# Turned down products in four experts stages, the recurrent layer's finish inside the cross attention, and query batches projected between first scores

## What is computed

```python
x = x + L0_attn(ln(x));  x = x + L0_xattn(ctx, ln(x), mask)      # "x0"
x = x + L0_ffn(ln(x))       # 8 experts, hidden 512, silu(gate) * up; "f0"
x = x + L1_attn(ln(x));  x = x + L1_xattn(ln(x), ctx)            # "x1"
x = x + L1_ffn(ln(x))       # one dense block, hidden 384, silu(gate) * up; "L1"
x = x + L2_attn(ln(x))      # recurrence over 512 steps, then ln(r) * gamma + beta
x = x + L2_xattn(ln(x), ctx, full mask)                          # "x2"
x = x + L2_ffn(ln(x))       # 8 experts, hidden 256, relu(g) * p, plus its own input; "f2"
x = x + L3_attn(ln(x));  x = x + L3_xattn(ln(x), ctx)
x = x + L3_ffn(ln(x))       # 8 experts, hidden 256, relu(x w1 + b1) w2 + b2; "f3"

# an expert: every token goes through every expert, the weight is 0 where it was not chosen
h  = act(x @ gate_w.T) * (x @ up_w.T)
eo = h @ down_w.T
out = out + coef[:, e] * eo
```

## Time and profile before

| | |
|---|---|
| median of 3 runs | 2433.44 us (2431.93 to 2447.59) |
| the profiled execution | 2440.75 us, span 2438.9 us |
| instructions | 36556 |
| PE | 2066.0 us, 85% of the span |
| DVE | 1662.4 us, 68% |
| ACT | 1045.7 us, 43% |
| POOL | 533.2 us, 22% |
| mean granted TensorE clock | 0.889 of full speed |

### The profile page before, as it was taken

The page is one execution under the profiler, slowest core; times in us unless marked ns, Lnnn a source line. Parts: engine busy times, 40 slices in busy tenths (PEclk is TensorE's granted clock), DMA queues, the critical chain, the costliest instruction groups (busy, mean ns, idle before and its releaser), DMA issues. The chain is left out here.

```text
span 2438.9 us, 36556 instructions
## 1 busy us (share of the span) xinstructions
PE 2066.0 (85%) x12192; PEld 1383.0 (57%) x12216; DVE 1662.4 (68%) x4273; ACT 1045.7 (43%) x2326; POOL 533.2 (22%) x905
## 2 busy tenths in 40 slices
PE   6698899998999897767774997598699979999888
PEld 3455788884555455433332554587334348777777
DVE  5666677786675576779997565456679856666655
ACT  2354222222564453455551344322367734444333
POOL 0342110102110530068883321010211010000010
PEclk8698899997897799889996798799689979999989
DMA  8321000004120420000003220000511110000000
GB/s 338 99 60 23 1 1 1 1 1 130 44 53 18 121 60 2 1 1 0 1 1 105 73 48 8 1 1 1 174 36 46 33 44 1 1 1 1 1 1 18
DMA packets 60073, 94.61 MB, mean 39 GB/s; under 512 B 11313, under 2 KB 33137, under 8 KB 58737
## 3 DMA queue, kind: packets, MB, share of 16 engines
q1 hardware_dynamic: 29312, 55.29, 6.7%
q0 software_dynamic: 29952, 36.45, 6.2%
q10 hardware_dynamic: 624, 0.54, 0.1%
HBM read 65.50 MB, written 31.29 MB: 40 GB/s over the span
## 5 line engine op out<-in xcount | busy, mean ns | idle before, releaser
L1008 DVE TENSOR_REDUCE m<-banks 128x1 f32<-128x512 f32 (+3 forms) x512 | 272.6, 584 | 94.6 <-PE banks L1172 54.4
L2687 PEld LDWEIGHTS banks<-w_ffn,eh 128*128 128x128 f32 x2144 | 279.2, 191 | 23.5 <-DVE eh L2628 1.9
L2687 PE MATMUL banks<-w_ffn,eh 128*128 128x128 f32 x2144 | 281.2, 274 | 1.5 <-DVE eh L2628 1.5
L1140 ACT ACTIVATE p<-banks 128x512 f32<-128x512 f32 (+3 forms) x512 | 234.0, 522 | 101.4 <-PE banks L1218 58.7
L1443 DVE TENSOR_REDUCE m<-banks 128x2 f32<-128x308 f32 x384 | 165.7, 475 | 137.1 <-PE banks L1743 70.3
L2675 PE MATMUL banks<-x_hi,w_hi 128*128 128x512 f32 x472 | 211.2, 447 | 17.4 <-PEq L332 17.4
L1170 PE MATMUL banks<-K,Qf 32*128 32x512 f32 (+2 forms) x512 | 182.5, 515 | 14.6 <-PEq L332 9.9
L2657 ACT ACTIVATE et<-banks 128x512 f32<-128x512 f32 x140 | 83.6, 597 | 246.8 <-PE banks L2677 203.2
L2677 PE MATMUL banks<-x_hi,w_lo 128*128 128x512 f32 x472 | 188.7, 400 | 0.0
L2676 PE MATMUL banks<-x_lo,w_hi 128*128 128x512 f32 x472 | 187.6, 397 | 0.0
L1216 PE MATMUL banks<-Q,K 32*128 32x512 f32 (+2 forms) x512 | 153.5, 499 | 14.9 <-ACT p L1140 13.0
(11 more groups left out here) (423 smaller groups left out, 4332.7 us busy)
## 6 DMA issues: line engine op xcount, KB each, us to landing
Qf<-stack_q_plain POOLq DMA_DIRECT2D x48, 256.0 KB, 3.0
Qf<-stack_q_masked POOLq DMA_DIRECT2D x32, 256.0 KB, 3.0
K<-stack_k_self POOLq DMA_DIRECT2D x32, 256.0 KB, 3.1
w_ffn<-ffn_dram SPq DMA_DIRECT2D x1, 6144.0 KB, 35.2
stack_q_plain<-q_hi SPq DMA_DIRECT2D x24, 256.0 KB, 3.1
stack_q_masked<-q_hi SPq DMA_DIRECT2D x16, 256.0 KB, 3.0
stack_k_self<-k_hi SPq DMA_DIRECT2D x16, 256.0 KB, 3.8
K<-stack_k_ctx POOLq DMA_DIRECT2D x48, 80.0 KB, 2.7
```

The source lines that it names most:

```text
L1008: ins = dve.reduce_max(k.m[:, t, h:h + 1], bank[:, 0:(t + 1) * P if k.kind == "page" else S], AX)
L1140: nc.scalar.activation(k.p[:, x % PBUFS, q0:S], score_banks[x % 3][:, q0:S], ACT.Exp).then_inc(sem("exp_done"), 1)
L2687: last = pe.matmul(bank[:, t * P:(t + 1) * P], k.h[:, n % RING, t * P:(t + 1) * P], w(down.format(e))[:, i * P:(i + 1) * P], start=(i == 0 ...
```

## The change

1. **Products turned.** In all experts stages `output(n)` takes the down weight as the stationary operand and h as the moving one, 512 tokens at once, with both split in a high and a low fp32r part: 3 matmuls an item. The sum over the tiles of a pair has the model dimension on partitions; ACT copies it out (`take_output`, in f3 with the bias as the activation's own), PE turns it back with 4 transposes into the same bank (`turn_output`), and DVE adds it to x. ACT writes the high part of h (`high`), GpSimd the low part (DVE in f3). GpSimd also cuts the down weights, and its cuts stand at fixed items among the low parts (`cuts`). The output lags 3 items instead of 2. The ring of split weights holds 2, 1, 4 and 3 experts; with two kinds and 2 tiles the hidden banks are 2 of each kind, not 3. In f2 the last 3 experts are taken batch by batch; L1 norms 1 batch ahead, not 2.
2. **Store by batch.** In f3 each batch is stored when its last expert has been added.
3. **The finish moved.** `scan_finish` is gone; in x2 GpSimd adds beta batch by batch and DVE multiplies and adds each batch before its norm (`add_scanned`).
4. **Later batches between first scores.** In all three cross attentions only batches 0 and 1 are normed before the first maximum; batches 2 and 3 are normed in pieces among the first maxima. PE turns batches 1, 2, 3 after chunks 1, 7, 13, projects 1 and 2 after chunks 4 and 10, and batch 3 after the chunks.

```diff
-        self.wring = 2 * tiles
+        self.wring = rings * tiles
+        self.d_hi, self.d_lo = sb("d_hi", [P, self.wring, P], F32R), sb("d_lo", [P, self.wring, P], F32R)
+        self.h_hi, self.h_lo = sb("h_hi", [P, HRING, S], F32R), sb("h_lo", [P, HRING, S], F32R)
...
+    def cuts(e, at):
+        if e >= apart:
+            return [(e + 1, at)] if lead == 1 and e == apart and at < tiles and e + 1 < experts else []
+        new = [(f, j) for f in range(1 if e == 0 else e + lead, e + lead + 1 + (e == apart - 1 and k.rings > 3)) if f < experts for j in range(tiles)]
+        late = 0 if e == 0 else 3
+        step = max(1, (B * tiles - late) // max(1, len(new)))
...
         @block.gpsimd
-            for e in range(1, experts):
-                cut_weights(net, pool, k, first, tiles, e, (e - 1) * tiles)
+            for i in range(tiles):
+                cut_down(net, pool, k, down, 0, i)
+            for n, (m, i) in enumerate(work):
+                if pool_lows:
+                    pool.wait_ge(sem("h_high"), n + 1)
+                    nc.gpsimd.tensor_tensor(k.h_lo[:, n % HRING], k.h[:, n % RING], k.h_hi[:, n % HRING].bitcast(F32), ALU.subtract).then_inc(sem("h_parts"), 1)
+                for new, j in cuts(e, b * tiles + i):
+                    cut_weight(net, pool, k, first, new, j, (new - 1) * tiles)
+                    cut_down(net, pool, k, down, new, j)
...
         @block.scalar          # for each item n, after the activation of item n
+                if n >= 1:
+                    high(n - 1)
+                if n >= TAKE and work[n - TAKE][1] == tiles - 1:
+                    take_output(work[n - TAKE][0])
...
         @block.tensor
-                for t in range(QT):
-                    last = pe.matmul(bank[:, t * P:(t + 1) * P], k.h[:, n % RING, t * P:(t + 1) * P], w(down.format(e))[:, i * P:(i + 1) * P],
-                                     start=(i == 0 and t == 0), stop=(i == tiles - 1), skip_group_check=True)
+                pe.matmul(y_bank[:], k.d_hi[:, at], h_hi, start=i == 0, stop=False)
+                pe.matmul(y_bank[:], k.d_lo[:, at], h_hi, start=False, stop=False)
+                pe.matmul(y_bank[:], k.d_hi[:, at], h_lo, start=False, stop=i == tiles - 1).then_inc(sem("h_used"), 1)
+            def turn_output(m):
+                pe.wait_ge(sem("y_taken"), m + 1)
+                for t in range(QT):
+                    last = pe.transpose(y_banks[m % ny][:, t * P:(t + 1) * P], k.y[:, t * P:(t + 1) * P], w("ident"))
-            for n in range(len(work) + 2):
+            for n in range(len(work) + LAG + 2):
                 if n < len(work):
                     hidden(n)
-                if n >= 2:
-                    output(n - 2)
+                if n >= LAG + 2 and work[n - LAG - 2][1] == tiles - 1:
+                    turn_output(work[n - LAG - 2][0])
+                if n >= LAG and n - LAG < len(work):
+                    output(n - LAG)
...
         # cross_block, DVE
+            if finish:
+                add_scanned(0)
             if not early:
                 vector_layernorm_of(dve, ch, net.x, k.n, 0, QT).then_inc(sem("xn_ready"), 1)
...
-            vector_layernorm_of(dve, ch, net.x, k.n, max(early, 1) * QT, B * QT).then_inc(sem("xn_ready"), 1)
+            if finish:
+                add_scanned(1)
+                vector_layernorm_of(dve, ch, net.x, k.n, QT, 2 * QT).then_inc(sem("xn_ready"), 1)
+                add_scanned(2)
+                ch.link(vector_layernorm_of(dve, ch, k.n.xn, k.n, (B - 1) * QT, B * QT))
+                add_scanned(3)
+            elif early <= 1:
+                vector_layernorm_of(dve, ch, net.x, k.n, QT, 2 * QT).then_inc(sem("xn_ready"), 1)
+            begun = max(early, 2)
...
                 maximum(c)
+                b, piece = divmod(c - 1, PIECES)
+                if 0 <= b < B - begun:
+                    vector_norm_piece(dve, ch, net.x, k.n, (begun + b) * QT, (begun + b + 1) * QT, piece)
...
         # cross_block, PE
-            normed(1)
-            project_queries(1)
             for c in range(nch + FIRST):
                 first_scores(c)
-                if c in (2, 7):
-                    normed(2 + c // 7)
-                if c in (5, 10):
-                    project_queries(2 + c // 10)
+                if c in (1, 7, 13):
+                    normed(1 + c // 6)
+                if c in (4, 10):
+                    project_queries(1 + c // 6)
+            project_queries(B - 1)
...
-        experts(None, None, "silu", ("L1_w", "L1_d"), 1, 3, norm_kind="one", ahead=2)
+        experts(None, None, "silu", ("L1_w", "L1_d"), 1, 3, rings=1, norm_kind="one", ahead=1)
...
-            scan_finish(net, k)
```

More of the change, by code:

```diff
@@ L1559, in values @@
                 pool.wait_ge(sem("v_ready"), (n + 1) * (GROUP + 1))
+            if finish:
+                for b in range(B):
+                    x = x_of(net, b)
+                    nc.gpsimd.tensor_tensor(x, x, over(w("m_beta"), 1, QT), ALU.add).then_inc(sem("with_offset"), 1)
             pool.memset(k.K[:, :, KPAD:].bitcast(F32), 0.0).then_inc(sem("zeroed"), 1)
@@ L2575, in experts_block @@
     pieces = DOUBLE_PIECES if norm_kind == "double" else PIECES
-    stretch = (experts - apart) * tiles
-    begin = apart * B * tiles + stretch + 2
+    stretch = max((experts - apart) * tiles, pieces)
+    begin = (apart * B + experts - apart) * tiles + LAG + 3
+    pool_lows = act_kind != "bias"
+    hidden_banks = 2 if tiles == 2 and k.kinds == 2 else 3
+    y_banks = ps[6:8] if tiles > 2 else ps[4:8]
+    ny = len(y_banks)
+    lead = min(2, k.rings - 1)
+    def cuts(e, at):
[4 more added lines that the diff above has]
+        step = max(1, (B * tiles - late) // max(1, len(new)))
+        c, rest = divmod(at - late, step)
+        return [new[c]] if rest == 0 and 0 <= c < len(new) else []
     with nc.Block() as block:
@@ L2631, in _ @@
-                if i == 1 and m >= 1:
-                    add_expert(m - 1)
-                b, piece = divmod(n - begin, max(stretch, pieces))
+                    hidden(n)
+                else:
+                    low(n)
+                if n >= LAG + 3 and work[n - LAG - 3][1] == tiles - 1:
+                    add_expert(work[n - LAG - 3][0])
+                b, piece = divmod(n - begin, stretch)
                 if 0 <= b < ahead and piece < pieces:
                     norm_piece(b, piece)
+            left = range((len(work) - LAG - 3) // tiles, len(pairs))
@@ L2645, in _, with high, take_output @@
         def _(act):
+            def high(n):
+                act.wait_ge(sem("h_ready"), n + 1)
+                if n >= HRING:
+                    act.wait_ge(sem("h_used"), n - HRING + 1)
+                nc.scalar.copy(k.h_hi[:, n % HRING], k.h[:, n % RING]).then_inc(sem("h_high"), 1)
+            def take_output(m):
+                act.wait_ge(sem("h_used"), tiles * (m + 1))
+                if m >= 1:
+                    act.wait_ge(sem("turned"), m)
+                e = pairs[m][0]
+                if act_kind == "bias":
+                    taken = nc.scalar.activation(k.y[:], y_banks[m % ny][:], ACT.Identity, bias=w("b2")[:, e:e + 1])
+                else:
+                    taken = nc.scalar.copy(k.y[:], y_banks[m % ny][:])
+                taken.then_inc(sem("y_taken"), 1)
             for n, (m, i) in enumerate(work):
```

218 lines of the change are left out of this document (120 added, 98 removed).

## The result

The changed kernel takes **2476.78 us** (median of 4 runs, 2461.78 to 2479.76) against 2432.68 of the kernel before in the same job: a ratio of **1.0155, 95% interval 1.0109 to 1.0202**. It is slower, by some 38 us by that ratio, which is worked out from all the runs; the two medians lie 44.1 us apart.

A forecast was written before the change was run, and what follows sets the result against it. PE was taken to bound the experts stages and first scores. Terms f0 +1.6, L1 and hand-over +2, f2 +9, f3 +25, x0 +10.5, x1 +7.5, x2 -3.8 gave +52 on 2433.4: 2485 us, range 2438 to 2508.

The forecast's parts named there:

- Part 2: In f3 PE waits at the turn for ACT's copy, 0.63 us a pair, +20 us; no wait in f0, L1, f2.
- Part 1: Turned product on PE, with four transposes a pair: f0 -6 us, L1 nothing, f2 +6, f3 +6.
- Part 3: GpSimd's cuts and low parts back up, so PE waits for the low part: f0 +2.8 us, f2 +2.5.
- Part 4: Stage ends: f0 +3.3 and +1.5 (norm pieces), f2 +0.4, f3 +1.4 and -2.3 (store), L1 hand-over +2 us.
- Part 5: Norm pieces, turns and projections among the first scores lengthen the cross attentions: x0 +10.5 us, x1 +7.5, x2 +7.
- Part 6: Finish moved into x2: its block's 13.3 us go, first scores begin 2.5 later; with x2's +7, -3.8 in all.
- no late turn: Rival: in f3 ACT starts its copy early enough, f3 pays 6 and not 26: 2465 us; chance 0.17.
- free turns: Rival: transposes vanish in PE's stream and ACT's copy is never waited for: 2409 us; chance 0.06.
- the slower product: Rival: the turned product is no faster than the old, 0.89 us an item: +51 us more; chance 0.03.
- First scores not set by DVE: Rival: only PE's added work counts, cross attentions give +1 in place of +14: 2472 us; chance 0.15.
- Norm pieces behind low parts: Rival: in f0's and f2's last quarter DVE's short operations wait for GpSimd: +20, 2505 us; chance 0.09.

The follow-up runs named there:

- run 3: The changed kernel, but in f3 ScalarE copies a pair's summed product before writing the high part of h: 2458.54 us, ratio 1.0103 against the kernel before.
- run 8: The kernel before with x2 alone changed (finish inside, later batches between first scores), store by batch, and L1 norming one batch ahead, not two: 2428.07 us.
- run 9: The kernel before once more, unedited, for a second profile: 2442.22 us.
- run 2: The changed kernel with batches 1 to 3 normed before the first maximum in all cross attentions, turns, projections and GpSimd's queue in changed order: 2468.30 us.
- run 10: The kernel before with f0's turned product, the finish inside x2 with later batches between first scores, and store by batch: 2425.88 us, ratio 0.9969.

## Why the prediction held, and where it did not

The forecast was 2485 and the sum +52; 2476.78 lies in the range, and the profile shows +39. So the sum is 13 too high, above all in f0 (+1.6 foreseen, -10.3 + 4.0 found) and f2 (+9 foreseen, +3.7 found), and terms too low elsewhere hide part of it. Step by step:

- **Part 2, the wait in f3**, is right in cause and size: 0.63 a pair foreseen, 0.66 measured in the pair above, and run 3 takes 15 us away by ACT's order alone.
- **Part 1, the pair's cost**, is mis-sized. It took 0.2325 for a matmul and 0.56 for the turn; measured are 0.227 and 0.41 + 0.08. (The 0.50 of the earlier trace rows ends at one more transpose, which has a wait of its own, so it can hold more than four transposes.) Made again: f0 36 x 0.227 + 0.49 = 8.66 against 9.12, f2 4.58 against 4.56, f3 3.21 against 3.17. So f0 -15 and not -6, f2 and f3 +1 and not +6 each. f0's -10.3 is that with 7.2 us of waits (next two steps), less 1.7 that the kernel before lost itself (291.3 against 31.75 x 9.12) and about 1 that I can't place; f2's +3.7 is nearly all waits, 1.7 and 1.9. The old item's price held the gaps of its own mix of matmuls, and I carried them into a stream that has none.
- **Part 3, GpSimd's backlog**: foreseen 2.8 and 2.5. In f0's steady part the waits of TensorE (line, releaser: us in total, times, longest) are

```profile
PE banks L2805 <- ACT ey L2741: 2.4, 2, 1.3
PE banks L2798 <- POOL h_lo L2650: 1.8, 3, 1.0
```

  These count from modelled ends and so come out low. By the starts of an item's last product (L2800), the items from 485.78 on, among the last cuts, take 2.47, 3.42 and 3.36 us in place of 2.04: the backlog costs 3.1 there, as foreseen, and 1.2 once more at f0's start. In f2 it costs 1.7. The two waits for the copy are not the backlog's, for they lie in the last expert, where GpSimd cuts nothing:

```profile
519.20 1.28 POOL L2650 TENSOR_TENSOR h_lo<-eh,h_hi 128x512 fp32r<-128x512 f32 x1 [0.77 <-ACT h_hi L2730]
519.30 1.21 DVE L406 TENSOR_TENSOR sq<-sq,vh 128x4 f32<-128x4 f32 x1
...
522.77 0.62 ACT L2730 CAST h_hi<-eh 128x512 fp32r<-128x512 f32 x1 [2.12 <-DVE eh L2694]
523.30 0.58 ACT L2741 COPY ey<-banks 128x512 f32<-128x512 f32 x1
...
523.93 0.66 PE L2805 MATMUL banks<-w_start,ey 128*128 128x128 f32 x4 [1.19 <-ACT ey L2741]
```

  A 4-element operation of a norm piece lasts 1.21 us and ends with GpSimd's low part; VectorE's next product for h is late, ACT waits 2.12 for it with the high part, and the copy that TensorE needs stands behind that. The second wait, at 542.70, looks the same. By item starts the two cost 2.9 us, where part 4 had 1.5 for the pieces and part 2 had said that f0 shows no wait for the copy.
- **Part 4**: f0's end +4.0 (foreseen +3.3). f3's end +0.4 (foreseen -0.9): the store gives 2.7 as said, but the chain costs 3.1, not 1.4. L1's +2 came, from the wrong cause: -1.5 for the batch and +3.6 for the product's end, for which I had put down nothing. Another 3.5 between L1 and x2 (-7.7 = -13.3 + 2.1 + 3.5) are the clock of run 8's windows and what follows them.
- **Part 5, first scores**: x0's stretch is 20.9 where 21.1 was counted (100.9 to 122.0), x1 +9.9 (foreseen +7.5: 6.5 in the stretch, the rest behind it), x2's stretch +6.5 (foreseen +7). In x0 the reason is right: VectorE is the path up to its last piece, and TensorE waits for it. That the end fits to 0.2 is luck: the last piece ends at 118.83 and not at 117.8, and turn, copy and projection behind it take 2.9 and not 4.2. (The earliest begin was also added wrongly, 97.41 + 2.7 is 100.1 and not 100.3; nothing hangs on it.)
- **Part 6**: the block was worth 13.3 to the tenth, x2 +8.8 (foreseen 9.5). The short operation behind GpSimd lasted 2.42, and the first scores begin 3.4 later (foreseen 2.5); that the memsets too stood in its way fits the rows above, but no run moves them.
- The stretch before f3 gave -5.4, which an unchanged kernel shows too (run 9), and no step had it. That much of a total read from one profile is luck.

Of the rivals, no late turn, free turns and the slower product are refuted: by 0.66 a pair, by 0.41 a turn, and by 2.04 an item. First scores not set by DVE is refuted by run 2 in x0 and in half of x1, but holds for the pieces in x2. Norm pieces behind low parts do occur, in small: 2.9 us in f0 and, with three such operations of 1.09 to 1.26 us among its last items, 1.9 in f2, together 4.8 of the rival's 20. No run takes the low parts off GpSimd, so how much of it is the hold alone isn't shown.

## What to carry to other kernels

When an engine is full and its order is fixed by hand, a handed-on copy costs by its place in the other engine's row: count that row to a tenth of a microsecond, and put what the full engine waits for first. A norm that lies under a wait for a load is free. Tied piece by piece to a loop of small chunks it can make its own engine the one that sets the loop, as VectorE in x0, however idle that engine looks on the mean. In x2, with more work ahead of the loop, the pieces cost nothing. Price a matmul stream by intervals of a stream of one kind, and undo the parts of a change one by one: here those that paid (0.3% together in run 10) were hidden under others that cost some 45 us.

## What the runs showed of the hardware

- fp32r matmuls of 512 columns start 0.227 us apart at full clock over nine and more in a row, whatever product they belong to; after fp32 transposes or the old fp32 product the first takes 0.31. Four 128x128 transposes take 0.41 in f0 and f3 and 0.36 in f2 (1712.02 to 1712.38); in the earlier trace rows it is 0.50, up to one more transpose with a wait of its own.
- VectorE's short operation can be held by GpSimd: 2.42 us from 1327.89, for a 4-element result, through an addition and the wide memsets behind it, and 1.21 us from 519.30 by one low part. Within a memset of the kernel before it took 0.17 (from 1314.36), so a memset alone doesn't always hold it.
- The time of one kernel follows its mean granted clock closely, 13.5 us for 0.01 (58 runs of the kernel before), and two profiles of it differ by 6 us in stages that nobody touched. A stage's length is only compared at like clock.
